# The order in which TensorE streams the moving columns of a mixture-of-experts feed-forward kernel: from straight through to halves by turns, pieces downwards and second half first

## What is computed

```python
q = x + embed[stage][..., None]
attn = softmax(q @ side^T) @ side                      # per sequence, 256 x 256
nx = attn * rsqrt(mean(attn^2) + 1e-6) * norm_w        # t, 8192 tokens x 256
weights = top 2 of softmax(t @ gate_w^T), normalised   # 8 experts
h1_e = t @ w1^T + 2 * (t @ a1_e^T) @ b1_e^T            # F = 1024, rank 16 per expert
h3_e = t @ w3^T + 2 * (t @ a3_e^T) @ b3_e^T
act_e = silu(h1_e) * h3_e
out_e = act_e @ w2^T + 2 * (act_e @ a2_e^T) @ b2_e^T
x + sum_e weights_e * out_e
```

## Time and profile before

| | |
|---|---|
| median of the runs shown | 1309.09 us (2 runs: 1308.8 and 1309.38) |
| the profiled execution's own time | 1308.66 us |
| its span, first to last instruction | 1306.9 us |
| TensorE matmul (PE) busy | 1301.1 us, 100% |
| TensorE weight load (PEld) busy | 1139.3 us, 87% |
| VectorE (DVE) busy | 843.5 us, 65% |
| ScalarE (ACT) busy | 527.5 us, 40% |
| GpSimd (POOL) busy | 249.9 us, 19% |
| granted TensorE clock | full, in all 40 slices of the span |
| DMA | 69.56 MB, mean 53 GB/s |

### The profile page before, as it was taken

The page is one execution under the profiler, slowest core; times in us unless marked ns, Lnnn a source line. Parts: engine busy times, 40 slices in busy tenths (PEclk is TensorE's granted clock), DMA queues, the critical chain, the costliest instruction groups (busy, mean ns, idle before and its releaser), DMA issues.

```text
span 1306.9 us, 18607 instructions
## 1 busy us (share of the span) xinstructions
PE 1301.1 (100%) x7286; PEld 1139.3 (87%) x7286; DVE 843.5 (65%) x1558; ACT 527.5 (40%) x991; POOL 249.9 (19%) x213
## 2 busy tenths in 40 slices
PE   9999999999999999999999999999999999999998
PEld 8999998888888888888888888888888888888887
DVE  6776656756665576656675667557675666565556
ACT  6776753333343344333333334333333343243332
POOL 3556540202011020202020202011020202020200
PEclk9999999999999999999999999999999999999999
DMA  9555810020202020201102020202020101102000
GB/s 294 145 147 154 233 43 33 2 73 2 73 2 73 1 73 1 59 16 33 42 2 73 1 73 2 73 1 74 2 73 1 57 17 35 40 1 73 1 17 17
DMA packets 71791, 69.56 MB, mean 53 GB/s; under 512 B 7050, under 2 KB 62744, under 8 KB 71576
## 3 DMA queue, kind: packets, MB, share of 16 engines
q1 hardware_dynamic: 71392, 68.37, 17.5%
q10 hardware_dynamic: 312, 0.02, 0.0%
HBM read 51.27 MB, written 17.10 MB: 52 GB/s over the span
## 4 chain that ended last, share of the span: by engine, by line
PE 98%; ACT 1%; DVE 0%; issue 0%; DVEq 0%
PE bank L1205 31%; PE bank L1204 31%; PE bank L1206 30%; PE bank L1330 2%; PE bank L1257 2%; PE bank L1308 1%; PE bank L1250 1%; ACT prob L663 0%; PE bank L1216 0%; ACT qT_hi L646 0%; ACT kT_hi L647 0%; DVE probT_lo L886 0%; DVE x_out L1148 0%; PE bank L1295 0%; ACT value_hi L657 0%
## 5 line engine op out<-in xcount | busy, mean ns | idle before, releaser
L1076 DVE TENSOR_TENSOR act_a<-silu_a,bank 128x512 f32<-128x512 f32 x128 | 87.7, 686 | 210.9 <-PE bank L1206 194.2
L754 ACT ACTIVATE br_hi<-act_br 128x512 fp32r<-128x512 f32 x128 | 81.0, 633 | 188.6 <-DVE act_br L1087 188.6
L747 ACT ACTIVATE silu_b<-bank 128x512 f32<-128x512 f32 x128 | 76.3, 596 | 187.9 <-PE bank L1206 187.0
L590 POOL TENSOR_TENSOR t_lo<-t_in,t_hi 128x512 fp32r<-128x512 f32 x32 | 40.6, 1291 | 552.2 <-ACT t_hi L734 552.2
L1205 PE MATMUL bank<-w2T_lo,s_hi 128*128 128x256 f32 x512 | 144.7, 283 | 0.0
L1206 PE MATMUL bank<-w2T_hi,s_lo 128*128 128x256 f32 x512 | 143.3, 280 | 0.0
L1204 PE MATMUL bank<-w2T_hi,s_hi 128*128 128x256 f32 x512 | 142.7, 279 | 0.0
L1084 DVE TENSOR_TENSOR act_b<-silu_b,bank 128x512 f32<-128x512 f32 x128 | 88.0, 688 | 81.4 <-PE bank L1206 80.4
L743 ACT ACTIVATE silu_a<-bank 128x512 f32<-128x512 f32 x128 | 75.8, 592 | 134.1 <-PE bank L1206 134.0
L609 POOL TENSOR_TENSOR v_lo<-v_full,v_hi 128x512 fp32r<-128x512 f32 x64 | 94.5, 1508 | 136.6 <-ACT v_hi L739 136.6
L1097 DVE TENSOR_TENSOR br_lo<-act_br,br_hi 128x512 fp32r<-128x512 f32 x128 | 104.7, 818 | 5.6 <-ACT br_hi L754 3.1
(11 more groups left out here) (197 smaller groups left out, 3242.2 us busy)
## 6 DMA issues: line engine op xcount, KB each, us to landing
kv<-in_fside_BxSxS SPq DMA_DIRECT2D x32, 256.0 KB, 3.3
x_in<-in_x SPq DMA_DIRECT2D x32, 256.0 KB, 4.0
t_scratch<-oT SPq DMA_DIRECT2D x32, 256.0 KB, 2.5
t_in<-t_scratch SPq DMA_DIRECT2D x16, 512.0 KB
x_out<-in_x SPq DMA_DIRECT2D x16, 512.0 KB, 4.0
out<-x_out SPq DMA_DIRECT2D x30, 256.0 KB, 4.0
rho<-scale_scratch SPq DMA_DIRECT2D x16, 256.0 KB
rstd<-scale_scratch SPq DMA_DIRECT2D x16, 256.0 KB
```

The costliest lines, as they stand in the source:

```text
L747: nc.scalar.activation(silu_b[:, :], h1_bank[j % 2][:, :], ACT.Silu).then_inc(silu_b_ready, 1)
L754: nc.scalar.activation(br_hi[j % 2][:, :], act_br[j % 2][:, :], ACT.Copy).then_inc(br_hi_ready, 1)
L1076: nc.vector.tensor_tensor(act_a[j % 2][:, :], silu_a[j % 2][:, :], h3_bank[j % 2][:, :], ALU.mult).then_inc(act_a_ready, 1)
```

## The change

No instruction is added, removed or moved, and none gets another semaphore. `product` gets an optional function `order` that rewrites the access patterns of the output and of the two parts of the moving operand in the same way; the stationary operand stays as it was. Two families of orders exist. `halves(piece)` cuts the columns into two halves and takes from the first and the second by turns, `piece` columns each time. `downwards(piece)` cuts the columns into pieces and takes the last piece first; within a piece the columns go upwards. `downwards(256)` of 512 columns and `downwards(128)` of 256 are simply the second half first. Each column still lands in its own place.

```diff
+            def halves(piece):
+                return lambda part: part.rearrange("p (a b c) -> p b a c", a=2, c=piece)
+
+            def downwards(piece):
+                return lambda part: part.rearrange("p (b c) -> p b c", c=piece)[:, ::-1]
+
-            def product(dst, w, x_parts, start, stop, grouped=True):
+            def product(dst, w, x_parts, start, stop, grouped=True, order=None):
                 (w_hi, w_lo), (x_hi, x_lo) = w, x_parts
+                if order:
+                    dst, x_hi, x_lo = order(dst), order(x_hi), order(x_lo)
...
             def low_rank(c):
-                                       dc == 0, dc == DC - 1)
+                                       dc == 0, dc == DC - 1, order=downwards(16))
...
             def first_expert(c, j):
+                for wT, bT, dst, k, done, w_order, b_order in (
+                        (w1T, b1T, h1_bank[j % 2], 0, h1_first, halves(8), halves(32)),
+                        (w3T, b3T, h3_bank[j % 2], 1, h3_first, halves(16), halves(64))):
...
             def second_expert(c, j):
+                    product(dst[:, :], at(bT, ALL, f), (v_hi[k][:, :], v_lo[k][:, :]), False, True, grouped=False,
+                            order=halves(32) if k == 2 else halves(64)).then_inc(done, 1)
...
             def down_y(c, j):
+                order = (None, halves(4), halves(8), halves(16), halves(32), halves(64), downwards(16), downwards(128))[j]
...
             def down_z(c, j):
+                product(sa_bank[:, :], at(a2T, ALL, j), at(s_at(c, j), ALL, ALL), j == 0, j == FC - 1,
+                        order=halves(128))
                 return product(ba_bank[:, :], at(a2T, ALL, j), (br_hi[j % 2][:, :], br_lo[j % 2][:, :]),
-                               j == 0, j == FC - 1)
+                               j == 0, j == FC - 1, order=downwards(256))
```

More of the change, by code:

```diff
@@ L1390, in first_expert @@
                 f = slice(j * P, (j + 1) * P)
-                for wT, bT, dst, k, done in ((w1T, b1T, h1_bank[j % 2], 0, h1_first),
-                                             (w3T, b3T, h3_bank[j % 2], 1, h3_first)):
+                for wT, bT, dst, k, done, w_order, b_order in (
+                        (w1T, b1T, h1_bank[j % 2], 0, h1_first, halves(8), halves(32)),
+                        (w3T, b3T, h3_bank[j % 2], 1, h3_first, halves(16), halves(64))):
                     if j == 0:
@@ L1395, in first_expert @@
                     for dc in range(DC):
-                        product(dst[:, :], at(wT, ALL, dc, f), (t_hi[c % 2][:, dc], t_lo[c % 2][:, dc]), dc == 0, False)
+                        product(dst[:, :], at(wT, ALL, dc, f), (t_hi[c % 2][:, dc], t_lo[c % 2][:, dc]), dc == 0, False,
+                                order=w_order)
                     if j == 0:
                         pe.wait_ge(v_lo_ready, v_count(c, k))
-                    product(dst[:, :], at(bT, ALL, f), (v_hi[k][:, :], v_lo[k][:, :]), False, True).then_inc(done, 1)
+                    product(dst[:, :], at(bT, ALL, f), (v_hi[k][:, :], v_lo[k][:, :]), False, True, order=b_order
+                            ).then_inc(done, 1)
             def second_expert(c, j):
@@ L1406, in second_expert @@
                 for bT, dst, k, done in ((b1T, h1_bank[j % 2], 2, h1_second), (b3T, h3_bank[j % 2], 3, h3_second)):
-                    product(dst[:, :], at(bT, ALL, f), (v_hi[k][:, :], v_lo[k][:, :]), False, True, grouped=False
-                            ).then_inc(done, 1)
+                    product(dst[:, :], at(bT, ALL, f), (v_hi[k][:, :], v_lo[k][:, :]), False, True, grouped=False,
+                            order=halves(32) if k == 2 else halves(64)).then_inc(done, 1)
             def y_block(k):
@@ L1414, in down_y @@
                 pe.wait_ge(down_in_ready, chunk_no(c, j) + 1)
+                order = (None, halves(4), halves(8), halves(16), halves(32), halves(64), downwards(16), downwards(128))[j]
                 for k in range(KT):
                     last = product(y_block(k), at(s_at(c, j), ALL, slice(k * P, (k + 1) * P)),
-                                   at(w2T, ALL, j), j == 0 and k % 2 == 0, False, grouped=False)
+                                   at(w2T, ALL, j), j == 0 and k % 2 == 0, False, grouped=False, order=order)
                 last.then_inc(y_done, 1)
@@ L1432, in down_z @@
                 pe.wait_ge(down_in_ready, chunk_no(c, j) + 1)
-                product(sa_bank[:, :], at(a2T, ALL, j), at(s_at(c, j), ALL, ALL), j == 0, j == FC - 1)
+                product(sa_bank[:, :], at(a2T, ALL, j), at(s_at(c, j), ALL, ALL), j == 0, j == FC - 1,
+                        order=halves(128))
                 return product(ba_bank[:, :], at(a2T, ALL, j), (br_hi[j % 2][:, :], br_lo[j % 2][:, :]),
-                               j == 0, j == FC - 1)
+                               j == 0, j == FC - 1, order=downwards(256))
             def finish_y(c, last_tile=False):
```

## The result

The changed kernel takes 1346.25 us (median of 2 runs, 1346.24 to 1346.26) against 1309.09: ratio 1.0284, 95% interval 1.024 to 1.0328. It is slower by 37 us, above the range of 1303 to 1330 us, and on the side of the first rival (1360 us).

A forecast was written before the change was run, and what follows sets the result against it. TensorE was taken as the bound, its matmul stream setting the time. The profiled 1308.7 us plus 0 for the jumps, with the median 0.4 us above that execution, gave 1309.0 us; range 1303 to 1330 us.

The forecast's parts named there:

- first rival: Each jump in the moving read or, more likely, the PSUM write loses one column's time: 52 us more, 1360 us; chance 0.08.
- I take zero, and the reason is rate: Jumps in the moving read cost 0: scattered weight loads need at most 1.47 ns per piece, the shortest piece lasts 1.69 ns.
- The upper bound of the same row: Scattered `w2_in` weight load, 188 against 140 ns, gives 0.375 ns per jump; over 122,484 moving-side jumps 46 us.
- The write to PSUM is the weaker half of the argument: Writing PSUM in pieces was also given zero cost, though no row shows such a write with jumps.
- Its marks: Signs of a cost per jump: w1T (63 jumps) grows by 27 ns to 253 ns, b3T (7 jumps) by 3 ns.
- The second rival: Each reordered matmul pays a second fixed part for setting up a three-step pattern: 5370 x 10 ns = 54 us, 1363 us; chance 0.05.
- The third: Only pieces of 8 and 4 columns are too short and halve the pace in w1T and `down_y`: 1517 us; chance 0.04.
- The fourth: The fixed part disappears if it comes from weight load and moving read meeting at each matmul's start: 1255 us; chance 0.05.
- the 10 ns of the fixed part: Estimated part of each matmul's time on TensorE beyond its columns: 226.7 - 512 x 0.423 = 10 ns, cause unknown.
- narrow sentence: Skill rule that every two neighbouring elements should be contiguous; pieces of at least 4 float32 fill a line, so cost zero.

The follow-up runs named there:

- all_h64: The changed kernel with halves by 64 in place of every other order, chunk 0 of down_y included: 1308.78 us, ratio 0.9997.
- write scan: Each tile streams its touched matmuls in one order, only the output reordered, moving operand read straight: 1309.06 us against 1308.73 for the kernel before.

## Why the prediction was wrong

- What bounds the kernel, and that every nanosecond of the stream passes into the end: right. The stretch of the tiles grew by 37.6 us and the time by 37.
- No instruction, wait or other engine matters: right; VectorE, ScalarE, GpSimd and the clock are unchanged. The counts of touched matmuls and of jumps stand too. One reading was not complete: not all large waits of VectorE and ScalarE are for TensorE's banks, as ScalarE's br_hi waits 188.6 us for VectorE's act_br. TensorE waits for neither, so nothing follows from it.
- "I take zero, and the reason is rate": this is the step that failed, the price of a jump in the moving read. It carried the pace of scattered weight loads over to the moving read with the words "if the moving side reads as the weight side does". It does not. A read by halves of 4 columns costs 23.3 ns per matmul and by 8 16.7 ns, though 1.69 and 3.4 ns per piece were more than the 1.47 ns that the weight side needs. A likely reason is that the weight load has slack (48 ns more per load and at most 5 ns of it in the stream) while the moving read has none; this is argued and not tested.
- The rows themselves say less than was taken from them. Straight weight loads of the float32r products take 188 or 189 ns as well, so 188 ns is not by itself the mark of a scattered load. And the scattered loads start 0.11 us apart (43.07, 43.18 and 43.30 us) just as the straight ones do (31.15, 31.26 and 31.37), so a load's duration is neither its pace nor a price per jump.
- The upper bound of the same row, 0.375 ns per jump or 46 us, was close: 37.6 us over 122,484 jumps is 0.31 ns each on average. That is luck. The price per jump is zero by 64 and by 128, 0.05 ns downwards by 4, 0.26 by 8 and 0.67 by 32, and by 1 it is below zero.
- "The write to PSUM is the weaker half of the argument", and the first rival's "more likely, the write": the other way round. The write cost nothing in any order down to pieces of two columns, the smallest tried.
- The first rival, a price at the jumps, was the right kind of cause and got 0.08. Its marks came out in part: w1T grew most, but by 15 of the 27 ns given, b3T by 6 where 3 were given, and a2T over br and s hardly; halves by 64 and by 128 are free by themselves.
- The second rival (set-up) is excluded by `all_h64`. The third (short pieces at half pace) appears only below the sizes of the change: by 2, 337 ns.
- The fourth, that another order could take the 10 ns of the fixed part away, was called unlikely, and for the change's own orders that is so. For single columns from two places its size came out: 226.7 to 215.8, 10.9 ns. Its reason, a meeting with the weight load, stays open: the place of the stationary operand does move the plain read, but only upwards, and a shorter load left 215.8 as it was and did not lower 226.7.
- The sentences on the Trainium skill: its rule in "PSUM — Partial Sum Buffer", section Specifications (TRN2), that any pattern that is not contiguous slows matmuls significantly, was given as the first rival's. On the PSUM side it does not hold here: 226.7 ns in every tile of the write scan. The Trainium skill's rule in "Advanced Engine Details and Errata", section Memory Cachelines, that accesses to the same 16-byte line run at full performance and another line at each access costs, does not tell the moving read either: halves by 4, whose pieces are 16 bytes long, take 250.0 ns, and halves by 1, which go 1 KB away at every column, take 215.8. The zero that the prediction drew from its narrow sentence failed with it on the read side.

What stays open: why the price falls in steps (most steady distances from 226.7 to 250.0 lie 3.33 ns or a multiple of it apart; quarters and eighths by 16, at 231.1 and 239.7, do not), why 64 columns per piece are free and 32 are not, why halves by 2 depend on the chunk, and why two places are read faster than one.

## What to carry to other kernels

A duration is not a pace, and a price taken from a resource with slack need not hold for one without; where the bound engine's own stream is touched and no row shows the new shape, put the weight on the nearest row's upper end and say so. Where a kernel is bound by TensorE with float32r operands, as this one is, it is worth trying to read the moving operand as single columns from its two halves by turns, write PSUM straight, and let the readers of PSUM undo the order with a stride of two; undoing it in writes to SBUF gave back 19 us here. Other types and widths were not tried. And a kernel that gives each tile its own variant prices fourteen of them in one run.

## What was not expected of the hardware

- A 512 wide float32r matmul takes 226.7 ns in a plain read and 215.8 with two places by turns, at any distance from 4 to 256 columns; a 256 wide one some 118 and 111.6. With four places it takes 283.3 ns, with eight 486.7, and every second column first takes 452.2.
- The write of a matmul to PSUM in pieces is free down to two columns (226.7 ns in all tiles of the write scan). Reading PSUM at every second column is free for VectorE (688 against 688 ns) and ScalarE (595 against 596 for silu_b). Writing SBUF to and fro is not: 1075 against 687 ns on VectorE (512 columns, 1 KB apart), 732 against 483 on ScalarE (256 columns, 512 bytes apart).
- The place where the stationary slice starts is worth up to 7.5 ns of a plain 512 wide matmul (226.7 to 234.2), repeats with 64 words, and is worth nothing with halves by 8.
